# An early-fusion model on one core: the roll layer in groups of 4, 4, 4, 4, 4, 4, 4, 2 and 2 images instead of eight groups of 4

## What is computed

```python
z = softmax(einsum('bse,he->bsh', x, W_A) * SCALING, axis=1)
zp = transpose(z, (0, 2, 1))
roll = zp[:, :, (i - j) % S] * (j <= i)
v = einsum('bse,fe->bsf', x, W_V).reshape(B, S, H, D)
out = einsum('bhij,bjhd->bihd', roll, v).reshape(B, S, E)
return einsum('bse,fe->bsf', out, W_O) + b_O
```

## Time and profile before

| | |
|---|---|
| Median of 3 runs | 1072.96 us |
| The profiled execution | 1074.8 us |
| Its span, first to last instruction | 1073.0 us |
| TensorE busy | 939.0 us, 88% |
| VectorE busy | 582.3 us, 54% |
| POOL busy | 519.4 us, 48% |
| ScalarE busy | 412.1 us, 38% |
| Mean granted TensorE clock | 0.936 |

### The profile page before, as it was taken

How to read it: one execution, slowest core, us unless ns; L and a number is a source line. 1 busy time by engine, 2 the same in 40 slices (tenths; PEclk the granted TensorE clock), 3 DMA queues, 4 the chain that set the end, 5 groups by cost and what they waited for, 6 DMA issues and landing times. The chain is left out here.

```text
span 1073.0 us, 29482 instructions
## 1 busy us (share of the span) xinstructions
PE 939.0 (88%) x10318; PEld 741.5 (69%) x10318; DVE 582.3 (54%) x1439; ACT 412.1 (38%) x1094; POOL 519.4 (48%) x714
## 2 busy tenths in 40 slices
PE   8699999978824999999999986599999954999996
PEld 6457777767722888888888875255665634888895
DVE  1768888855995677533333325678877432111111
ACT  2357667743334343443434311233333222333331
POOL 0045565620603777777677617777772002343332
PEclk9879999979967999999999989789999976999998
DMA  7010000002003988887888723335463047466750
GB/s 253 2 44 2 0 0 0 1 2 84 1 0 109 307 267 271 279 243 214 254 261 253 231 80 103 103 104 140 122 214 125 21 153 261 138 224 236 282 154 25
DMA packets 79820, 149.28 MB, mean 139 GB/s; under 512 B 18892, under 2 KB 53327, under 8 KB 75760
## 3 DMA queue, kind: packets, MB, share of 16 engines
q1 hardware_dynamic: 34768, 77.15, 21.4%
q0 software_dynamic: 17712, 47.88, 15.7%
q10 hardware_dynamic: 27248, 23.09, 6.4%
HBM read 200.22 MB, written 31.73 MB: 216 GB/s over the span
## 5 line engine op out<-in xcount | busy, mean ns | idle before, releaser
L1311 POOL DMA_INDIRECT x_x<-m_x_rows,x_idx x170 | 165.8, 975 | 75.2 <-issue 35.9
L1337 PE MATMUL x_pup<-x_xt,x_w 128*128 128x128 f32 (+1 forms) x2176 | 184.7, 251 | 0.0
L1337 PEld LDWEIGHTS x_pup<-x_xt,x_w 128*128 128x128 f32 (+1 forms) x2176 | 168.7, 166 | 6.0 <-issue 5.9
L1606 POOL DMA_INDIRECT rl_y<-m_y_rows,rl_idx x136 | 132.8, 976 | 46.3 <-issue 36.9
L1407 DVE TENSOR_TENSOR x_hid<-x_gate,x_pup 128x128 f32<-128x128 f32 x170 | 48.9, 288 | 148.3 <-ACT x_gate L1379 144.3
L1351 PE MATMUL x_pdown<-x_w,x_hid 128*128 128x256 f32 (+1 forms) x408 | 104.2, 389 | 0.3 <-DVE x_y L1414 0.3
L1375 ACT ACTIVATE x_xt<-x_pturn 128x256 f32<-128x256 f32 x170 | 65.3, 384 | 88.9 <-PE x_pturn L1322 86.0
L434 POOL TENSOR_TENSOR wa_probs<-wa_probs,wa_peak 68x544 f32<-68x544 f32 x64 | 69.9, 1092 | 58.7 <-DVE wa_peak L576 58.7
L2365 DVE TENSOR_TENSOR x_y<-x_pdown,x_b 128x256 f32<-128x256 f32 x21 | 8.9, 425 | 151.3 <-PE x_pdown L2321 151.3
L2351 ACT ACTIVATE x_hid<-x_pup,x_b 128x128 f32<-128x128 f32 (+1 forms) x200 | 52.9, 356 | 93.3 <-PE x_pup L2304 93.1
L1379 ACT ACTIVATE x_gate<-x_pup 128x128 f32<-128x128 f32 x170 | 47.2, 278 | 93.5 <-PE x_pup L1337 92.8
(11 more groups left out here) (329 smaller groups left out, 1886.8 us busy)
## 6 DMA issues: line engine op xcount, KB each, us to landing
x_w<-in_experts SPq DMA_DIRECT2D x204, 384.0 KB
late_w<-in_w SPq DMA_DIRECT2D x28, 1024.0 KB, 14.5
m_y_rows<-x_y ACTq DMA_DIRECT2D x170, 128.0 KB
xT<-in_w SPq DMA_DIRECT2D x12, 1024.0 KB, 6.2
xn<-in_w SPq DMA_DIRECT2D x10, 1024.0 KB, 10.7
h<-in_w SPq DMA_DIRECT2D x10, 1024.0 KB, 14.7
m_x_rows<-xn SPq DMA_DIRECT2D x34, 128.0 KB, 1.9
x_x<-m_x_rows,x_idx POOLq DMA_INDIRECT x170, 3.1
```

The costliest lines, as they stand in the source:

```text
L1311: nc.gpsimd.indirect_dma_start(x[:, s, :], None, x_rows, bass.IndirectOffsetOnAxis(ap=idx[:, s:s + 1], axis=0))\
L1337: mm = nc.tensor.matmul(pup[rows:rows + wide, bank, m * P + side * wide:m * P + (side + 1) * wide], w[:, lane, first:first + wide], xt[:, ...
L1606: nc.gpsimd.indirect_dma_start(y[:, t % YR, kk, :], None, y_rows, bass.IndirectOffsetOnAxis(ap=idx[:, n:n + 1], axis=0))\
```

## The change

The sizes of the groups become a list, seven of 4 and two of 2, so NG = 9 and there are 12 steps, 0 to 11. What had been computed from g (tiles, pairs, columns, semaphore counts) comes from running sums of the list. Loops over the two pairs of a group become loops over `halves(g)`, one pair for a group of two. The last groups have the tiles: group 6 in 13, 14 and out 12, 13; group 7 in 15 and out 14; group 8 in 16 and out 15, 16. No group has three outward tiles any more, and `pairs_out` goes; a group has one projection and one addition. The drain's list has 3 fillers behind each inversion instead of 4 and 2. Over the whole layer TensorE issues 170 fillers instead of 162.

```diff
-    GI = 4
-    NG = B // GI
+    GI, PAIR = 4, 2
+    SIZES = [4] * 7 + [2] * 2
+    NG = len(SIZES)
+    FROM = [sum(SIZES[:g]) for g in range(NG + 1)]
...
     def tiles_in(g):
-        return list(range(0 if g == 0 else 2 * g + 1, 2 * g + 3))
+        return list(range(-(-FROM[g] * S // P), -(-FROM[g + 1] * S // P)))
     def tiles_out(g):
-        return list(range(2 * g, NT if g == NG - 1 else 2 * g + 2))
-    def pairs_out(g):
-        ts = tiles_out(g)
-        return [(ts[n] // 2, ts[n:n + 2]) for n in range(0, len(ts), 2)]
+        return list(range(FROM[g] * S // P, FROM[g + 1] * S // P))
+    def halves(g):
+        return range(SIZES[g] // PAIR)
+    def pair_of(g, p):
+        return FROM[g] // PAIR + p
...
                 def mix_logits(g):
-                        mm = nc.tensor.matmul(pz[0:H, 0:GC], late["w_a"][:, c, :], xT[:, c, g * GC:(g + 1) * GC],
+                        mm = nc.tensor.matmul(pz[0:H, 0:SIZES[g] * S], late["w_a"][:, c, :], xT[:, c, cols_of(g)],
...
                     if has2:
                         forward(g2, 0, 0)
                         forward(g2, 0, 1)
-                        forward(g2, 1, 0)
+                        for p in halves(g2)[1:]:
+                            forward(g2, p, 0)
...
                     if has2 and not has1:
                         fill(g2 + 1, 8)
-                        invert(g2, 0)
-                        fill(g2 + 1, 4)
-                        invert(g2, 1)
-                        fill(g2 + 1, 2)
-                        for m, ts in pairs_out(g2):
-                            project(g2, m, ts)
+                        for p in halves(g2):
+                            invert(g2, p)
+                            fill(g2 + 1, 3)
+                        project(g2)
...
                     if has1:
-                        values(g1, 1)
+                        for p in halves(g1)[1:]:
+                            values(g1, p)
...
                     if has2:
-                        invert(g2, 1)
-                        fill_values(g1, 2)
+                        for p in halves(g2)[1:]:
+                            invert(g2, p)
+                            fill_values(g1, 2)
...
                 def add_projected(g):
-                    dve.wait_ge(projected, m + 1)
+                    ts = tiles_out(g)
+                    dve.wait_ge(projected, g + 1)
```

More of the change, by code:

```diff
@@ L1476, in roll_layer @@
     inv = [k["const"]("inv_re"), k["const"]("inv_neg"), k["const"]("inv_im"), k["const"]("inv_im")]
-    GI = 4
-    NG = B // GI
+    GI, PAIR = 4, 2
+    SIZES = [4] * 7 + [2] * 2
+    assert sum(SIZES) == B
+    NG = len(SIZES)
+    FROM = [sum(SIZES[:g]) for g in range(NG + 1)]
     GC = GI * S
-    CP = 2 * S
+    CP = PAIR * S
     YR = 4
@@ L1490, in tiles_out, with pairs_through, cols_of @@
             return []
-        return list(range(2 * g, NT if g == NG - 1 else 2 * g + 2))
-    def pairs_out(g):
-        ts = tiles_out(g)
-        return [(ts[n] // 2, ts[n:n + 2]) for n in range(0, len(ts), 2)]
+        return list(range(FROM[g] * S // P, FROM[g + 1] * S // P))
[3 more added lines that the diff above has]
+        return FROM[g] // PAIR + p
+    def pairs_through(g):
+        return FROM[g + 1] // PAIR
+    def cols_of(g):
+        return slice(FROM[g] * S, FROM[g + 1] * S)
+    assert all(len(tiles_out(g)) <= 2 for g in range(NG))
     STEPS = NG + 3
@@ L1630, in values @@
                 def values(g, p):
-                    j = g * 2 + p
+                    j = pair_of(g, p)
                     if j:
@@ L1641, in forward @@
                 def forward(g, p, part):
-                    n = (g * 2 + p) * 2 + part
-                    pe.wait_ge(v_moved, g * 2 + p + 1)
+                    n = pair_of(g, p) * 2 + part
+                    pe.wait_ge(v_moved, pair_of(g, p) + 1)
                     if n >= 3:
@@ L1650, in turn_mix @@
                     pe.wait_ge(z_normed, g + 1)
-                    for b in range(GI):
+                    for b in range(SIZES[g]):
                         mm = nc.tensor.transpose(pz[0:S, b * H:(b + 1) * H], z[:, b, :], ident[0:H, 0:H])
@@ L1657, in forward_mix @@
                     for part in range(2):
-                        mm = nc.tensor.matmul(pz[0:NF, (1 + part) * GI * H:(2 + part) * GI * H], fwd[part],
-                                              zt[:, :, :].rearrange("s b m -> s (b m)"), start=True, stop=True)
+                        at = (1 + part) * GI * H
+                        mm = nc.tensor.matmul(pz[0:NF, at:at + SIZES[g] * H], fwd[part],
+                                              zt[:, 0:SIZES[g], :].rearrange("s b m -> s (b m)"), start=True, stop=True)
                     mm.then_inc(zf_done, 1)
                 def invert(g, p):
-                    j = g * 2 + p
+                    j = pair_of(g, p)
                     pe.wait_ge(terms, (j + 1) * 4)
@@ L1675, in invert, with project @@
                     mm.then_inc(inverted, 1)
-                def project(g, m, ts):
-                    pe.wait_ge(out_moved, 2 * (g + 1))
-                    if m:
-                        pe.wait_ge(proj_added, m)
-                    for s, t in enumerate(ts):
+                def project(g):
+                    pe.wait_ge(out_moved, pairs_through(g))
+                    if g:
+                        pe.wait_ge(proj_added, g)
+                    for s, t in enumerate(tiles_out(g)):
                         nc.tensor.matmul(pr[:, s, :], ident, late["b_o"][:, :], start=True, stop=False)
@@ L1787, in _ @@
                     if has2:
-                        invert(g2, 1)
-                        fill_values(g1, 2)
+                        for p in halves(g2)[1:]:
+                            invert(g2, p)
+                            fill_values(g1, 2)
                     if has1:
                         turn_mix(g1)
-                    for m, ts in pairs_out(g2):
-                        project(g2, m, ts)
+                    if has2:
+                        project(g2)
                     if has1:
@@ L1874, in _ @@
                     if has2 and not has1:
-                        move_out(g2, 0)
-                        move_out(g2, 1)
+                        for p in halves(g2):
+                            move_out(g2, p)
                         root("out", outs)
@@ L1895, in _ @@
                     if has1:
-                        move_values(g1, 1)
+                        for p in halves(g1)[1:]:
+                            move_values(g1, p)
                         exp(g1)
                     if has2:
-                        move_out(g2, 0)
-                        move_out(g2, 1)
+                        for p in halves(g2):
+                            move_out(g2, p)
                     if has1:
@@ L1993, in _ @@
                         scale("in", tiles_in(g1))
-                    for m, ts in pairs_out(g3):
-                        add_projected(m, ts)
+                    if outs:
+                        add_projected(g3)
                     if has2 and not has1:
-                        multiply(g2, 0)
-                        multiply(g2, 1)
+                        for p in halves(g2):
+                            multiply(g2, p)
+                        dve.wait_ge(proj_added, g3 + 1)
                         for t in outs:
-                            dve.wait_ge(proj_added, t // 2 + 1)
                             measure("out", t)
```

41 lines of the change are left out of this document (24 added, 17 removed).

## The result

| | before | after |
|---|---|---|
| Median | 1073.12 us (10 runs, 1071.03 to 1074.47) | 1075.72 us (10 runs, 1074.60 to 1077.79) |
| The profiled execution | 1074.8 us | 1074.76 us |
| Its span | 1073.0 us | 1073.0 us |
| Mean granted TensorE clock | 0.936 | 0.941 |

The ratio is 1.0027, with an interval of 1.0017 to 1.0037: the change costs 1.8 to 4.0 us, most likely 2.9 (the two medians differ by 2.6). Predicted were 1076.3 us, a range of 1074.4 to 1078.6, and slower at 0.80.

What follows compares the result with a forecast made beforehand. TensorE's list of products was taken to bound the step. The end's pieces summed to 45.57 us against 41.25, +4.32; one store pair less, -0.99, gave +3.3 on the median 1072.96: 1076.3 us, range 1074.4 to 1078.6.

Steps and rivals of the forecast that it cites:

- Step 8: Last step before the new one, now with two images in its first half: 19.01 us instead of 22.2.
- Step 9: The new, extra step: TensorE's list of 13.21 us plus 1.55 us of waiting, 14.76 us.
- Step 10 to the last addition: The drain, from its forward products through fillers, one inversion and the projection to the addition: 9.21 us.
- Addition to normalisation: From the last addition to the start of the last normalisation: 2.59 us instead of 2.84.
- The two waits: TensorE waits at the new step's outward turns, for ScalarE's normalisation (0.70 us) and its move out of PSUM (0.85 us).
- Two stores less: Behind the last normalisation of two tiles instead of three, one pair of stores less: -0.99 us.
- The landing: SyncE's wait after the last store stays at 3.3 us; a microsecond's difference would count against the prediction.
- The weight load and the moved combining: First two experts' weights loaded one step later, and VectorE's combining of tiles 15 and 16 moved to step ends: 0.
- The base: The difference of +3.3 us is added to the median of the runs, 1072.96, not to the profiled execution, 1074.8.
- The halved drain: Rival: the drain halves and the new step is cheap, giving 1065.6 us, faster; chance 0.05.
- The vanishing waits: Rival: TensorE's waits at the new step's outward turns vanish, +1.8 us, 1074.7, no measurable change; chance 0.14.
- The falling clock: Rival: TensorE's clock falls to the 1.2 GHz level in the new steps, about 1085.5 us; chance 0.06.

## Why the prediction was right

- *Step 8*: 19.01 predicted, 19.03 measured. *Step 9*: 14.76, measured 14.60. *Step 10 to the last addition*: 9.21, measured 869.49 - 860.28 = 9.21. *Addition to normalisation*: 2.59, measured 872.18 - 869.49 = 2.69. The sum was +4.32 and is +4.27. That it agrees to 0.05 us is luck in part, since errors of up to 0.36 us cancel.
- *The two waits* were sized at 0.70 and 0.85, together 1.55 us over a full step. Counted in the same way they were 0.65 and 0.54, together 1.19, and the list was 14.60 - 1.19 = 13.41 instead of 13.21; the errors, -0.36 and +0.20, cancel in part. Most of the 0.20 is the half of the mixture's turn and of the projection: it saved 2.70 - 1.40 = 1.30 (rl_pr takes 841.90 to 844.60 in step 8, 857.80 to 859.20 in step 9), where I had 1.46. Both waits stand where the prediction put them, for the reasons that it gave: the first turn came at 5.57 us into the step (5.56 predicted). The second is smaller since the moves of two images' logits overlap with the values' (0.26 us long, with the next start 0.16 us behind), where I had taken those of four, and one after the other. That they were the waits of VectorE's order and ScalarE's queue is shown by the run that scaled first: the first vanished and the step became 0.86 us shorter.
- *Two stores less*: -0.99 predicted, -0.98 measured.
- *The landing* was the sign that failed: I said that it stays at 3.3 us and that a difference of a microsecond would speak against me. It was 2.2. But the 3.3 belonged to that one execution of the kernel before and not to six stores, which landed in 2.3 us elsewhere. Since I had kept the term the same on both sides, the sum lost nothing by it. The split by the Trainium skill, DMA: Bandwidth & Descriptors, section Anatomy of one DMA, which gave 0.4 less for four stores, is not borne out as a part that grows with their number: 2.3 for six against 2.2 to 2.7 for four. A fixed part of about 2 us is near these rows, but not near the 1.3 to 1.5 us of the three kernels where only rows of x stood last.
- *The weight load and the moved combining* were costed at 0. For the load a run shows it. For the combining the lengths do: step 7 has 22.19 us in both kernels, and step 8 has 19.03 where 19.01 had been counted without it.
- *The other signs* held: no earlier step changed, the granted clock was 1.00 in steps 8 to 10, and the stage behind the layer took 195.8 us against 196.0.
- *The base*: adding the difference to the median, not to the profiled execution, was needed. That execution's landing and its 48 first products were 1.0 and 0.8 us longer than in the drain without fillers, which has the same stores and the same first products (3.3 against 2.3, 8.03 against 7.22); together that is about what it lay above the median, an argument from two rows rather than a test.
- *The rivals.* The halved drain is out: steps 9 and 10 up to the last normalisation took 14.60 + 11.90 = 26.5 us, I had counted 26.6, and 21.1 was the point of decision. The vanishing waits did not come, and when 0.86 of their 1.19 us was taken away, the time did not move by what can be measured. The falling clock did not come in the changed kernel, but I had its reason wrong. I argued from the idle time of the drain before, as though idle time alone counted; of the fillers that I had called a cost of 3.2 us, some are what kept the clock up beside those waits, and the ones that can have done it are the six ahead of the inversion. The Trainium skill, TensorE: Matmul & The Clock Gate, section HAM oscillation — how this bites in real kernels, has idle gaps between groups of products as the cause. The rows agree in that the clock fell when the waits grew to 2.02 us in all, none of them longer than 1.05; at 1.15 us in all it fell only where fillers were missing too.

## What to carry to other kernels

This pipeline's drain does not halve with the size of its last group: the extra step still owes the older group's work, and it runs into waits that a full step covers. Put the short group where the engine waits for data anyway, price the end step by step, and compare profiles by step lengths rather than by ends. Before filler products are taken out, take out the waits beside them: here the other order brought nothing or a loss, since the clock fell. How far that holds for other lengths and places of waits is not shown.

## What was not expected of the hardware

The same 1.15 us of waits went with a granted clock of 1.00 with ten fillers behind them and with 0.61 without, though only two of the ten stand ahead of where it fell. After the fall it stayed below 1.00 into the next step even with TensorE busy for 5.00 of 5.00 us (0.71 in 860 to 865 us). The inversion that ran in it, whose start is 855.15 us, took 3.06 us instead of 2.12.

The wait for the last stores' landing was 2.2 to 2.7 us in the ten profiles where all these stores stand behind the last normalisation, four or six, the changed kernel's among them, and 3.3 in the one of the kernel before. What made that one long is open. Where only rows of x stood last, it was 1.3 to 1.5 us in three profiles, although a store of x and one of h carry the same 128 KB; what makes this difference is open too.
